# Leaving out the products with a sequence's empty state in a fused Mamba-2 and routed-attention kernel, with PSUM banks given out as pairs or singles

## The chip, the cores and the metric

One core of a Trainium2 chip runs the whole kernel. The time is the device time of one execution in microseconds (us), lower is better. Engines are named as in the profile: PE is the matrix engine (PEld its weight loads), DVE the vector engine, ACT the scalar engine, POOL the general one, SP the queue that issues most DMAs.

## The reference

Eight sequences of 1024 tokens, 512 wide. After a layer norm, two branches are added to the input: a Mamba-2 block and a routed attention. Cut to what matters for the change:

```python
def step(state, inp):                      # one token
    dA_t, dt_t, x_t, B_t, C_t = inp
    state = state * dA_t[:, :, None, None] + (dt_t[:, :, None] * x_t)[..., None] * B_t[:, None, None, :]
    y = jnp.einsum('bhpn,bn->bhp', state, C_t)
    return (state, y)
init = jnp.zeros((Bsz, NHEADS, HEADDIM, D_STATE), x.dtype)
_, ys = jax.lax.scan(step, init, xs_scan)
y = ys.transpose(1, 0, 2, 3) + D[None, None, :, None] * xs
y = y.reshape(Bsz, L, D_INNER) * jax.nn.silu(z)
y = y * jax.lax.rsqrt(jnp.mean(y * y, -1, keepdims=True) + EPS) * gamma
return x + y @ out_proj_w.T
```

The state is zero at the start of each sequence, and what it is after a sequence's last token is used by nothing.

## The kernel before, in words

The program has two halves, one after the other. The Mamba half comes first; the attention half follows, and the change does not touch its code.

**Blocks and chunks.** The 8192 tokens are 16 blocks of 512 (`NBLK`), each of 4 chunks of 128 (`CK`), so 64 chunks (`NCH`), eight to a sequence (`TPS`). Block i+1 is prepared while the chunks of block i run: its rows are normed and turned (`turn`), its router logits and step sizes made (`logits`, `dt`, `cum`), and ten convolutions done (`conv`: products on PE, `raw`, `tap0` and a tanh on ACT, three taps (L1412) and the last product `conv_silu` (L1418) on DVE, into the tile xsT).

**One chunk.** The PE steps are: `open` (L1046 and L1050, transposes of xsT), `inter` (L1086, state times C: what the sequence so far gives to this chunk), `proj` of the chunk before (L1104), `intra` (L1114, the chunk with itself), `gram` of the next chunk (L1057), `z` of the next chunk in two halves (L1067 and L1069), `state` (L1095, what this chunk adds to the state), `gate` (L1076, transposes of the gated result). Between `intra` and `gate` lies a chain on three engines, called the y chain below: `y2` (L1482, DVE), `yz` (L1488, DVE), `square` (L1857, ACT), `mean` (L1492, DVE), `root` (L2016, POOL), `y_high` (L1861, ACT), `y_low` (L1496, DVE). Beside them stand `y_in` (L1461, DVE, takes `inter`'s result), `y_skip` (L2012, POOL), `decayed` (L2007, POOL, the old state times its decay), `xw` (L2000, POOL), and `state_out` (L1469, DVE, adds the product `state` to the decayed state; at a sequence's end L1471 writes zeros instead).

**What sets the order.** Every engine runs its own list in order and waits on semaphores. The lists come from a planner that runs while the kernel is built: `make_plan` weaves the steps of PE (`back` with the convolutions and turns of later blocks, at shares that `Part` and `CONV_START, CONV_END` set), and `arrange` hands them with costs in microseconds and dependencies to `Order`, which places the steps of the other engines by due times and gives each PE step its PSUM banks. Before the change, `Order` keeps the eight banks apart: banks 0 to 3 are two pairs, for `open`, `inter`, `intra`, `state` and `gate`; banks 4 to 7 are singles. A PE step that gets a bank waits until the last reader of that bank's former content is done (`wait_given_back`).

## Time and profile before

| what | value |
|---|---|
| runs | 4119.1, 4124.62, 4128.99 us (median 4124.62) |
| profiled execution, its own time | 4083.68 us |
| its span | 4082.2 us |
| PE, DVE, ACT, POOL busy | 89%, 74%, 63%, 45% of the span |
| PE weight loads busy | 53% |
| Mamba half | to about 2008 us |
| top-k search between the halves | to about 2116 us |
| attention half | 1966 us, from there to the end |

The span runs from the first instruction to the last. A busy PE row has a modelled end, so how long a step occupies PE is read from start to start. What stands in square brackets behind a row of the timeline is how long its engine was idle before it, and whose work ended that.

### The profile page before, as it was taken

The page shows a single profiled execution, that of the slowest core. Times are in us where ns is not written, and L with a number is a line of the kernel's source. Part 1 is how long each engine was busy: PE and PEld are TensorE (multiplying, and loading weights), DVE is VectorE, ACT ScalarE, POOL GpSimd, SP SyncE. Part 2 cuts the span into 40 slices and gives each one's busy share as a digit, 9 for nine tenths or more (in the row PEclk, how much of TensorE's full clock was granted, in tenths as well). Part 3 has the DMA queues.
Part 4 walks back from the last instruction along what each step waited for, and adds up shares of the span by engine and source line. Part 5 has one row for each costly group of instructions (what it writes and reads, how often), then busy time and mean ns, then how long its engine had stood idle before and what let it go on. Part 6 is the DMA issues. An engine that isn't in the chain of part 4 may idle for free.

```text
span 4082.2 us, 72578 instructions
## 1 busy us (share of the span) xinstructions
PE 3651.9 (89%) x28414; PEld 2154.2 (53%) x28414; DVE 3024.5 (74%) x5404; ACT 2557.8 (63%) x4781; POOL 1830.9 (45%) x1513
## 2 busy tenths in 40 slices
PE   4899999999999999999518899998999989999998
PEld 2455555555555555555305555555555556555555
DVE  4887888888888888877567576776777667777773
ACT  4776676776676767765314666666666566666665
POOL 0232333333333333333214777756555565555455
PEclk8899999999999999999759999999999999999998
DMA  4223232323232233222222433334333343333332
GB/s 124 63 71 78 55 73 71 83 71 84 71 75 59 71 74 76 79 68 44 49 42 66 100 70 75 72 73 101 72 75 65 77 97 68 70 75 75 67 66 37
DMA packets 297669, 294.28 MB, mean 72 GB/s; under 512 B 38663, under 2 KB 223623, under 8 KB 295280
## 3 DMA queue, kind: packets, MB, share of 16 engines
q1 hardware_dynamic: 241008, 186.70, 18.0%
q0 software_dynamic: 56320, 102.94, 14.4%
q8 instruction: 225, 3.69, 0.4%
q14 instruction: 116, 0.95, 0.1%
HBM read 176.19 MB, written 101.71 MB: 68 GB/s over the span
## 4 chain that ended last, share of the span: by engine, by line
PE 62%; DVE 15%; DMA 8%; ACT 6%; issue 5%; POOL 3%; SPq 1%; POOLq 0%; DVEq 0%; ACTq 0%
PE pair L1021 8%; PE pair L1104 7%; PE pair L1267 6%; PE pair L1067 6%; PE pair L1114 5%; DMA xin<-x 3%; PE pair L1184 3%; PE pair L1159 3%; PE pair L1086 3%; DMA rbc<-rank 3%; PE pair L1172 2%; PE pair L1095 2%; PE pair L1200 2%; PE pair L1146 2%; PE pair L1046 2%
## 5 line engine op out<-in xcount | busy, mean ns | idle before, releaser
L1412 DVE SCALAR_TENSOR_TENSOR cv<-raw,taps,cv 128x512 f32<-128x512 f32 x480 | 407.5, 857 | 60.7 <-ACT cv L1809 59.4
L1651 DVE TENSOR_REDUCE smx<-pair 128x2 f32<-128x514 f32 x512 | 346.8, 685 | 140.6 <-PE pair L1200 140.5
L2078 POOL TENSOR_TENSOR ph<-pf,ph 128x512 f16<-128x512 f32 x256 | 323.9, 1268 | 201.5 <-ACT ph L1942 200.2
L1021 PE MATMUL pair<-xhT,whi 128*128 128x512 f16 x1280 | 382.8, 381 | 3.4 <-DVE zs L1454 2.7
L2083 POOL TENSOR_TENSOR ohl<-of,ohl 128x256 f16<-128x256 f32 x256 | 209.3, 818 | 307.9 <-ACT ohl L1947 307.9
L1267 PE MATMUL pair<-whi,oT 128*128 128x512 f16 x1024 | 330.8, 385 | 1.1 <-ACT xq L1903 1.1
L1067 PE MATMUL pair<-whi,xhT 128*128 128x512 f16 x1024 | 327.4, 381 | 2.5 <-ACT raw L1795 2.5
L1590 DVE TENSOR_SCALAR_CACHE_REDUCE rjunk<-rbc,cst 128x640 f16<-128x640 f16 (+1 forms) x192 | 185.5, 966 | 181.8 <-DMA rbc<-rank 179.4
L1104 PE MATMUL pair<-ohi,yT 128*128 128x512 f16 x1024 | 316.5, 381 | 1.1 <-ACT yT L1866 1.1
L1159 PE MATMUL pair<-xq,whi 128*128 128x512 f16 x1024 | 312.7, 388 | 0.7 <-ACT xk L1903 0.7
L1839 ACT ACTIVATE de<-de,cum 128x128 f32<-128x128 f32 x1024 | 312.1, 389 | 1.5
L1939 ACT ACTIVATE pf<-pair 128x1024 f32<-128x1024 f32 x256 | 262.7, 1026 | 44.1 <-PE pair L1229 34.3
L1684 DVE TENSOR_TENSOR ph<-pf,ph 128x512 f16<-128x512 f32 x256 | 277.6, 1085 | 6.0 <-ACT ph L1942 3.8
L1942 ACT CAST ph<-pf 128x1024 f16<-128x1024 f32 x256 | 267.5, 1045 | 8.2
L2007 POOL TENSOR_TENSOR state<-state,decs 128x1024 f32<-128x1024 f32 x63 | 138.8, 2204 | 265.7 <-issue 264.3
L2051 POOL DMA_INDIRECT gat<-rows,slot_i x192 | 185.7, 967 | 155.6 <-DVE slot_i L1600 113.9
L2072 POOL DMA_INDIRECT y<-res,slot_i x128 | 203.3, 1588 | 112.6 <-ACT res L1960 92.9
L1021 PE MATMUL pair<-xhT,wlo 128*128 128x512 f16 x640 | 243.6, 381 | 0.0
L1245 PE MATMUL pair<-nvb,pnT 96*128 96x65 f16 x1024 | 202.0, 197 | 45.7 <-DVE qa L1615 37.4
L1114 PEld LDWEIGHTS pair<-xdt,de 128*128 128x128 f32 x2048 | 237.7, 192 | 7.8 <-issue 0.8
L1247 PE MATMUL pair<-vhi,ph 128*128 128x65 f16 x2048 | 241.5, 195 | 0.0
L1249 PE MATMUL pair<-vhi,ph 128*128 128x65 f16 x2048 | 241.4, 195 | 0.0
(245 smaller groups left out, 10446.9 us busy)
## 6 DMA issues: line engine op xcount, KB each, us to landing
de<-cum SPq DMA_DIRECT2D x64, 1024.0 KB, 9.4
rows<-rowt SPq DMA_DIRECT2D x16, 1040.0 KB, 12.6
xin<-x SPq DMA_DIRECT2D x16, 1024.0 KB, 12.8
y<-xin SPq DMA_DIRECT2D x16, 1024.0 KB, 4.3
y<-ob POOLq DMA_DIRECT2D x64, 256.0 KB, 4.1
rbc<-rank SPq DMA_DIRECT2D x64, 256.0 KB, 3.6
qb<-qa SPq DMA_DIRECT2D x32, 512.0 KB
wst<-wkv SPq DMA_DIRECT2D x32, 256.0 KB, 3.3
```

The lines of the kernel that those rows point to most:

```text
L1021: ins = pe.matmul(bk[:], w[:, k, ws], xt[:, ha, k, :], start=n == 0, stop=n == 3 * KD - 1)
L1067: pe.matmul(pz[:], xt[:, ha, k, cs], w[:, k, j * 512:(j + 1) * 512], start=n == 0, stop=False)
L1104: ins = pe.matmul(bk[:], yT[:, ha * KI + k, :], w[:, k, :], start=k == 0 and n == 0, stop=k == KI - 1 and n == 2)
L1114: ins = pe.matmul(pw[:, h * HD:(h + 1) * HD], de[ch % 2][:, h, :], xdt[:, h, :], start=True, stop=True)
L1159: ins = pe.matmul(bk[:], w[:, k, ws], xq[:, ha * KD + k, :], start=n_ == 0, stop=n_ == 3 * KD - 1)
L1267: ins = pe.matmul(bk[:], o_[:, ha * KD + k, :], w[:, k, 3 * D:4 * D], start=k == 0 and m == 0, stop=k == KD - 1 and m == 2)
L1412: ve.scalar_tensor_tensor(c_[:], r_[:, t:t + BLK], taps[:, ct, t:t + 1], c_[:], ALU.mult, ALU.add).then_inc(done, 1)
L1651: ve.tensor_reduce(smx[:, qt, 2 * h2:2 * h2 + 2], sc[:, :, 0:NK + 1], AX.X, ALU.max)
L1684: ve.tensor_tensor(p_[:, 1, 0], f[:, 0], p_[:, 0, 0], ALU.subtract).then_inc(S.plv, 1)
L1839: ins = ac.activation(d_[:, h, :], d_[:, h, :], ACT.Relu, bias=cum_t[i % 2][:, c, h:h + 1], scale=-1.0)
L1942: ac.copy(p_[:, 0], f[:]).then_inc(S.ph, 1)
L2078: po.tensor_tensor(p_[:, 1, 1], f[:, 1], p_[:, 0, 1], ALU.subtract).then_inc(S.plp, 1)
```

## The change

A sequence's first chunk (`opens`) no longer has the steps `inter`, `y_in`, `y_skip` and `decayed`: its `y2` adds the product `intra` to the skip term (dxs) at once, and its `state_out` copies the product `state`. A sequence's last chunk (`ends`) no longer has `xw`, `decayed`, `state` and the write of zeros. The counts that semaphores are waited for follow (`fed`, `kept`, `both`). In numbers: 8 of 64 `inter`, 7 of 63 `state`, 8 `y_in`, 8 `y_skip`, 7 `xw`, 15 of 63 `decayed` and 8 writes of zeros fall away.

`Order` may now give any even-odd pair of the eight banks as a pair and any bank as a single; a single prefers a bank whose partner is taken. The share of the convolutions and of the turns in a block is shifted, and the length of a block is now the sum of its own steps.

```diff
-CONV_START, CONV_END = -0.15, 1.1
+CONV_START, CONV_END = -0.05, 1.05
...
-                sets = [(k, k + 1) for k in range(0, BANKS // 2, 2)] if kind == "pair" else [(k,) for k in range(BANKS // 2, BANKS)]
+                sets = [(k, k + 1) for k in range(0, BANKS, 2)] if kind == "pair" else [(k,) for k in range(BANKS)]
...
-                b = min(sets, key=lambda b: max(banks[k][0] for k in b))
+                b = min(sets, key=lambda b: (len(b) == 1 and b[0] ^ 1 not in busy and b[0] ^ 1 not in taken, max(banks[k][0] for k in b)))
...
+def opens(ch):
+
+    return ch % TPS == 0
...
+def ends(ch):
+
+    return (ch + 1) % TPS == 0
...
-            yield ("inter", ch)
-            yield 1.72
+            if not opens(ch):
+                yield ("inter", ch)
+                yield 1.72
...
-                yield ("state", ch)
-                yield 1.72
+                if not ends(ch):
+                    yield ("state", ch)
+                    yield 1.72
...
-            others.append(Part(ahead, 0.5 if i else 0, 2.6))
+            others.append(Part(ahead, 0.5, 2.6) if i else Part(ahead, 0.3, 4.0))
...
-        weave(Feed(back(i), CK * 21.6, record), *others)
+        weave(Feed(back(i), sum(us for us in back(i) if isinstance(us, float)), record), *others)
...
-                ve.memset(state[0][:], 0.0).then_inc(S.new, 1)
...
             def state_out(ch):
                 new = state[(ch + 1) % 2]
-                q.wait_ge(S.st_mm, ch + 1)
-                q.wait_ge(S.sd, ch + 1)
-                if (ch + 1) % TPS:
-                    ve.tensor_tensor(new[:], new[:], bank("state", ch)[:].rearrange("p (h d) -> p h d", h=NH), ALU.add).then_inc(S.new, 1)
+                q.wait_ge(S.st_mm, kept(ch) + 1)
+                got = bank("state", ch)[:].rearrange("p (h d) -> p h d", h=NH)
+                if opens(ch):
+                    q.wait_ge(S.inter_mm, fed(ch))
+                    ve.tensor_copy(new[:], got).then_inc(S.new, 1)
                 else:
-                    ve.memset(new[:], 0.0).then_inc(S.new, 1)
+                    q.wait_ge(S.sd, both(ch) + 1)
+                    ve.tensor_tensor(new[:], new[:], got, ALU.add).then_inc(S.new, 1)
...
-                ve.tensor_tensor(yb[:], yb[:], bank("intra", ch)[:].rearrange("p (h d) -> p h d", h=NH), ALU.add).then_inc(S.y2, 1)
+                if opens(ch):
+                    q.wait_ge(S.yl, ch)
+                    q.wait_ge(S.dxs, ch + 1)
+                else:
+                    q.wait_ge(S.yd, fed(ch) + 1)
+                ve.tensor_tensor(yb[:], dxs[:] if opens(ch) else yb[:], bank("intra", ch)[:].rearrange("p (h d) -> p h d", h=NH), ALU.add).then_inc(S.y2, 1)
```

The change moves instructions too. Three places are shown, first PE at the end of chunk 40, the first chunk of the sixth sequence, as it was: `state`, `gate`, `open` of chunk 41 and its `inter`, one behind the other, then the first row of `proj`.

```order
3173 L1021 MATMUL pair<-xhT,wlo 128x512
3174 L1095 MATMUL pair<-xw,btok 128x512 x2
3175 L1076 MATMUL pair<-id,yhl 128x128 x16
3176 L1046 MATMUL pair<-cst,xsT 128x128 x8
3177 L1050 MATMUL pair<-cst,xsT 128x128
3178 L1086 MATMUL pair<-state,xsT 128x512 x2
3179 L1104 MATMUL pair<-ohi,yT 128x512
```

The same place of the changed kernel, whose lines stand 38 lower in the file: `state` (L1133), `cum`, `gate` (L1114), a convolution (L1059, of which the eight rows are cut to two), `open` (L1084, L1088), `inter` (L1124).

```order
3159 L1133 MATMUL pair<-xw,btok 128x512 x2
3160 L1069 MATMUL pair<-dts,cst 128x16 x4
3161 L1074 MATMUL pair<-cst,dts 16x128 x4
3162 L1114 MATMUL pair<-id,yhl 128x128 x16
3163 L1059 MATMUL pair<-xhT,whi 128x512 x2
3164 L1059 MATMUL pair<-xhT,wlo 128x512
...
3171 L1084 MATMUL pair<-cst,xsT 128x128 x8
3172 L1088 MATMUL pair<-cst,xsT 128x128
3173 L1124 MATMUL pair<-state,xsT 128x512 x2
```

`cum` and a convolution now lie between `state` and the next `open`, which still gets the pair that `state` held. In all, 21 of the 64 `open` get the pair of the `state` before them; with one exception, in the first block, something besides `gate` lies between the two. The other 43 get a pair that other steps held earlier.

The second place is PE at the end of chunk 39, the last of the fifth sequence. Before: the end of `z`, `state`, a `turn`, `gate`, and the start of `logits` (L1008), behind which come `gram`, `open`, `inter`.

```order
3076 L1069 MATMUL pair<-z_bias,ones 128x512
3077 L1095 MATMUL pair<-xw,btok 128x512 x2
3078 L996 MATMUL pair<-id,xh 128x128 x8
3079 L1076 MATMUL pair<-id,yhl 128x128 x16
3080 L1008 MATMUL pair<-shi,xhT 128x24
```

After: `z`, `logits` (L1046 there, 33 rows cut to two), `gate` (L1114), `gram` (L1095), `open`, `proj` (L1142).

```order
3066 L1107 MATMUL pair<-z_bias,ones 128x512
3067 L1046 MATMUL pair<-shi,xhT 128x24
...
3099 L1046 MATMUL pair<-shi,xhT 128x24
3100 L1114 MATMUL pair<-id,yhl 128x128 x16
3101 L1095 MATMUL pair<-xsT 128x128
3102 L1084 MATMUL pair<-cst,xsT 128x128 x8
3103 L1088 MATMUL pair<-cst,xsT 128x128
3104 L1142 MATMUL pair<-ohi,yT 128x512
```

`state` and `inter` are gone, `logits` stands ahead of `gate` instead of behind it, and the last convolution, which stood between `intra` 39 and `z`, now stands ahead of `intra` 39. Between `intra` 39 and `gate` 39 there are now `z`, a turn, `z` and `logits` alone.

The third place is DVE at the same boundary, from `yz` of chunk 39 on, before:

```order
1219 L1488 SCALAR_TENSOR_TENSOR yb<-yb,zs 128x1024
1220 L1412 SCALAR_TENSOR_TENSOR cv<-raw,taps,cv 128x512
1221 L1492 TENSOR_SCALAR yn<-yn 128x1
1222 L1412 SCALAR_TENSOR_TENSOR cv<-raw,taps,cv 128x512 x2
1223 L1418 SCALAR_TENSOR_TENSOR xsT<-xsT,cv 128x512
1224 L1496 SCALAR_TENSOR_TENSOR yhl<-yb,yn,yhl 128x1024
1225 L1412 SCALAR_TENSOR_TENSOR cv<-raw,taps,cv 128x512
1226 L1471 MEMSET state 128x1024
1227 L1454 SCALAR_TENSOR_TENSOR zs<-zs,pair 128x512
1228 L1418 SCALAR_TENSOR_TENSOR xsT<-xsT,cv 128x512
1229 L1449 TENSOR_TENSOR gmask<-pair,cst 128x128
1230 L1369 TENSOR_SCALAR logit<-pair,nrm 128x8 x4
```

And after, where L1407 and L1408 read the result of `logits`, L1542 is `y_low` and L1456 `conv_silu`:

```order
1147 L1534 SCALAR_TENSOR_TENSOR yb<-yb,zs 128x1024
1148 L1450 SCALAR_TENSOR_TENSOR cv<-raw,taps,cv 128x512
1149 L1456 SCALAR_TENSOR_TENSOR xsT<-xsT,cv 128x512
1150 L1538 TENSOR_SCALAR yn<-yn 128x1
1151 L1456 SCALAR_TENSOR_TENSOR xsT<-xsT,cv 128x512
1152 L1494 SCALAR_TENSOR_TENSOR zs<-zs,pair 128x512
1153 L1407 TENSOR_SCALAR logit<-pair,nrm 128x8 x4
1154 L1408 SCALAR_TENSOR_TENSOR dts<-pair,dt_b 128x64
1155 L1542 SCALAR_TENSOR_TENSOR yhl<-yb,yn,yhl 128x1024
1156 L1494 SCALAR_TENSOR_TENSOR zs<-zs,pair 128x512
1157 L1416 SCALAR_TENSOR_TENSOR dts<-dts 128x64
1158 L1469 TENSOR_TENSOR decs<-de,cum 128x16
```

The last `conv_silu` of the block stands further ahead, and `y_low` stands behind the two instructions that need the result of `logits`.

On SP, in the blocks that open a sequence, the load of the rows for the block after next (L2122) stood behind the load for the decays of the next block's third chunk (L2141) and now stands right behind the store (L2126) on which it waits. In the attention half the order of all PE steps is unchanged; some get another bank than before.

## Rows read from the trace of the kernel before

**Rows 1.** The page: busy us, share of the span and instructions of each engine.

```profile
PE 3651.9 (89%) x28414; PEld 2154.2 (53%) x28414; DVE 3024.5 (74%) x5404; ACT 2557.8 (63%) x4781; POOL 1830.9 (45%) x1513
```

**Rows 2.** Windows: stretch, its length, busy us by engine, PEclk, DMA share, GB/s.

```profile
851.00:1084.00 233.00, 226.05 (x1368) 128.40 (x1368) 194.35 (x269) 164.38 (x365) 82.14 (x52) 1.00 0.30 73
1820.00:2010.00 190.00, 167.46 (x897) 94.64 (x895) 119.59 (x121) 92.12 (x199) 51.37 (x34) 0.95 0.21 38
```

**Rows 3.** Waits of PE from 120 to 1990 us: total us, times, longest.

```profile
PE pair L1046 <- DVE state L1469: 33.4, 45, 3.2
PE pair L1046 <- DVE xsT L1418: 32.5, 16, 12.7
PE pair L1076 <- DVE yhl L1496: 10.1, 4, 4.7
```

**Rows 4.** Timeline of PE: start, us, engine, line, operation, idle time before it.

```profile
143.39 1.97 PE L1046 MATMUL pair<-cst,xsT 128*128 128x128 f32 x8 [12.73 <-DVE xsT L1418]
1378.71 1.09 PE L1046 MATMUL pair<-cst,xsT 128*128 128x128 f32 x8 [0.42 <-DVE state L1469]
```

**Rows 5.** Timeline of PE from chunk 7's `intra` to chunk 8's `proj`.

```profile
368.35 0.59 PE L1021 MATMUL pair<-xhT,whi 128*128 128x512 f16 x2
...
370.94 0.38 PE L1067 MATMUL pair<-whi,xhT 128*128 128x512 f16 x1
...
373.94 0.62 PE L996 MATMUL pair<-id,xh 128*128 128x128 f16 x8
...
377.40 1.99 PE L1095 MATMUL pair<-xw,btok 128*128 128x512 f32 x4
379.23 0.61 PE L996 MATMUL pair<-id,xh 128*128 128x128 f16 x8
379.67 1.06 PE L1076 MATMUL pair<-id,yhl 128*128 128x128 f16 x16
380.57 0.18 PE L1008 MATMUL pair<-shi,xhT 128*128 128x24 f16 x1
...
381.77 0.47 PE L1057 MATMUL pair<-xsT 128*128 128x128 f32 x2
...
384.26 1.88 PE L1086 MATMUL pair<-state,xsT 128*128 128x512 f32 x4
385.98 0.38 PE L1104 MATMUL pair<-ohi,yT 128*128 128x512 f16 x1
```

**Rows 6.** Instructions of `inter` on PE: count, ns min/median/max.

```profile
L1086 PEld LDWEIGHTS pair<-state,xsT x256: 186/191/338, 145.2 to 1982.0; 128*128 128x128 f32 x128
```

**Rows 7.** Timeline from 1344 to 1353 us, chunks 40 and 41.

```profile
1344.08 2.47 DVE L1337 BATCH_NORM_STATS2 stats<-xin 128x6 f32<-128x512 f32 x4 [3.00 <-DMA xin<-x]
1348.34 1.09 PE L1046 MATMUL pair<-cst,xsT 128*128 128x128 f32 x8 [3.19 <-DVE state L1469]
1349.38 3.58 PE L1086 MATMUL pair<-state,xsT 128*128 128x512 f32 x4
```

**Rows 8.** A window behind that wait; PEclk is the third number from the end.

```profile
1350.00:1352.00 2.00, 2.00 (x4) 0.76 (x3) 1.93 (x6) 1.53 (x4) 1.35 (x2) 0.50 0.00 0
```

**Rows 9.** Timeline: y chains of chunks 38 and 63, and readers of `logits`.

```profile
1271.73 1.17 PE L1114 MATMUL pair<-xdt,de 128*128 128x64 f32 x9
...
1274.50 1.21 DVE L1482 TENSOR_TENSOR yb<-yb,pair 128x1024 f32<-128x1024 f32 x1
1283.34 1.28 DVE L1496 SCALAR_TENSOR_TENSOR yhl<-yb,yn,yhl 128x1024 f16<-128x1024 f32 x1 [0.17 <-ACT yhl L1861]
...
1317.29 0.61 DVE L1369 TENSOR_SCALAR logit<-pair,nrm 128x8 f32<-128x8 f32 x4
1317.83 0.21 DVE L1370 SCALAR_TENSOR_TENSOR dts<-pair,dt_b 128x64 f32<-128x64 f32 x1
...
1991.74 1.22 DVE L1482 TENSOR_TENSOR yb<-yb,pair 128x1024 f32<-128x1024 f32 x1 [7.41 <-PE pair L1114]
...
1998.79 1.89 PE L1076 MATMUL pair<-id,yhl 128*128 128x128 f16 x16 [7.08 <-DVE yhl L1496]
```

More of the change, by code:

```diff
@@ L295, in run, with fed, kept, both @@
         plan.now = now
+def opens(ch):
+    return ch % TPS == 0
+def ends(ch):
+    return (ch + 1) % TPS == 0
+def fed(ch):
+    return ch - (ch + TPS - 1) // TPS
+def kept(ch):
+    return ch - ch // TPS
+def both(ch):
+    return sum(1 for c in range(ch) if not opens(c) and not ends(c))
 def chain(*gens):
@@ L381, in last, with state_before @@
         return step if step[1] >= 0 else None
+    def state_before(ch):
+        return last(("state", ch - 2 if ends(ch - 1) else ch - 1))
     def conv_of(i, k):
@@ L405, in arrange @@
         elif name == "inter":
-            add("PE", 1.72, step, [last(("state_out", a - 1))], [("pair", [("y_in", a)])])
+            add("PE", 1.72, step, [("state_out", a - 1)], [("pair", [("y_in", a)])])
         elif name == "state":
@@ L458, in arrange @@
         add("DVE", 2.6, ("mask", ch), [("decay", ch), ("gram_out", ch)])
[L459 to L465 removed]
+        add("ACT", 0.25, ("open_b", ch), [("open", ch), state_before(ch)])
+        add("DVE", 1.22, ("xdt", ch), [("open", ch), last(("intra", ch - 1))] + ([] if ends(ch - 1) else [("xw", ch - 1)]))
+        add("DVE", 1.22, ("dxs", ch), [("open", ch), last(("y2" if opens(ch - 1) else "y_skip", ch - 1))])
+        if not ends(ch):
+            add("POOL", 2.0, ("xw", ch), [("xdt", ch), ("dec", ch), state_before(ch)])
+            if not opens(ch):
+                add("POOL", 2.5, ("decayed", ch), [("dec", ch), ("state_out", ch - 1)] + ([] if opens(ch - 1) else [("inter", ch - 1)]))
+                add("DVE", 1.22, ("state_out", ch), [("state", ch), ("decayed", ch), ("inter", ch)])
+            else:
+                add("DVE", 1.22, ("state_out", ch), [("state", ch), last(("inter", ch - 1))])
         for j in range(2):
@@ L468, in arrange @@
             add("DVE", 0.69, ("z_silu", ch, j), [("z_tanh", ch, j)])
-        add("DVE", 1.22, ("y_in", ch), [("inter", ch), ("cum_exp", i), last(("y_low", ch - 1))])
-        add("POOL", 2.7, ("y_skip", ch), [("y_in", ch), ("dxs", ch)])
-        add("DVE", 1.22, ("y2", ch), [("intra", ch), ("y_skip", ch)])
+        if opens(ch):
+            add("DVE", 1.22, ("y2", ch), [("intra", ch), ("dxs", ch), last(("y_low", ch - 1))])
+        else:
+            add("DVE", 1.22, ("y_in", ch), [("inter", ch), ("cum_exp", i), ("y_low", ch - 1)])
+            add("POOL", 2.7, ("y_skip", ch), [("y_in", ch), ("dxs", ch)])
+            add("DVE", 1.22, ("y2", ch), [("intra", ch), ("y_skip", ch)])
         add("DVE", 1.23, ("yz", ch), [("y2", ch), ("z_silu", ch, 0), ("z_silu", ch, 1)])
@@ L524, in back @@
             yield 1.26
[L525 to L526 removed]
+            if not opens(ch):
+                yield ("inter", ch)
+                yield 1.72
             if ch:
```

47 lines of the change are left out of this document (23 added, 24 removed).

## The prediction

> **What bounds the kernel now.** I read the page's head first, then windows by stage, then PE's waits, then the timeline at the waits. Of the span of 4082.2 us the page has PE busy for 89%, DVE for 74% [rows 1]; the windows [rows 2] split that. A sequence in the middle of the Mamba half (233 us) has PE busy for 226.05 us, DVE for 194.35, ACT for 164.38, POOL for 82.14, at full clock: PE is the bound there, and 7 us a sequence are its idle time. The stretch with the last block (190 us, PE 167.46) has PE waiting too, and the attention half is untouched code.
>
> What PE waits for [rows 3] is nearly all in front of `open` (L1046): 33.4 us in 45 waits for `state_out`, and 32.5 us in 16 waits for the last `conv_silu`. The first is not a data dependence: `open` reads xsT, but it gets the pair of banks that `state` wrote and `state_out` still reads. Its usual size is 0.42 us [rows 4]; where it is larger, DVE stood before a load of rows, as at 1344 us: 3.00 us for xin, then `state_out`, and `open` 3.19 us late [rows 7]. Of the second kind 12.73 us is the start-up [rows 4], where ten convolutions in a row are bound by DVE and ACT; the 15 others sum to 32.5 - 12.7 = 19.8 us, 1.3 each on average.
>
> One rule speaks against counting PE's busy time. PE's weight loads are busy for 128.40 of 233 us only [rows 2]. The Trainium skill, "Perfetto Trace Analysis", section Identifying the Most-Contended Engine, holds that matmul busy share is no good measure and that weight loads are one; taken so, `inter` would cost only its four loads of 0.191 us [rows 6], 0.8 us, and 15 removed products 11.5 us. The trace disagrees: `inter` starts at 384.26 and the next product at 385.98 [rows 5], so 1.72 us of PE's order passes. I count that.
>
> **The change part by part.** All terms are for the profiled execution (4083.68 us, span 4082.2) and are then put on the median.
>
> *Products gone from PE.* `state` takes 379.23 - 377.40 = 1.83 us, `inter` 1.72 [rows 5]. Seven of each: 12.8 and 12.0. The eighth `inter`, in the start-up, took 3.58 us or so at the low clock (as the one at 1349.38 did [rows 7]), but without it PE reaches `intra` sooner and waits there for `xdt` and the mask: between 0 and 3.6, I take 1.5. Sum **-26.3**.
>
> *Work gone from DVE and POOL* (`y_in`, the writes of zeros, `decayed`, `xw`, `y_skip`): nothing, since these engines are covered by PE (194.35 and 82.14 beside 226.05 us [rows 2]). Where that cover is thin, at a boundary, it is in the terms below.
>
> *Waits for `state_out`.* With all eight banks in one pool, 43 `open` get other pairs, and 20 of the other 21 have a convolution, `cum` or `logits` beside `gate` between `state` and themselves. A convolution is 370.94 - 368.35 = 2.6 us, `logits` 381.77 - 380.57 = 1.2 us [rows 5], both more than the 0.42 missing. The rows' load moves ahead on SP by a chunk or more, so the large ones should go too. At least nothing, at most 33.4; I take **-30**.
>
> *Waits for `conv_silu`.* At a sequence's start the last convolution is now ahead of `intra`, and `conv_silu` further ahead on DVE; inside a sequence the distance on PE is as before, but ACT and DVE reach it sooner in their lists. Between 0 and 19.8; I take **-15**. The 12.73 us of the start-up I leave.
>
> *A new wait at a sequence's end.* This is what is late next. Between the end of `intra` and `gate` PE had a convolution, `z`, a turn, `z`, `state` and a turn: 379.67 - 368.35 = 11.3 us. Now it has `z` (373.94 - 370.94 = 3.0), a turn with the second `z` (377.40 - 373.94 = 3.46) and `logits` (1.2) [rows 5]: 7.7 us. The y chain needs 1998.79 - 1991.74 = 7.05 us with nothing beside it, and 1284.62 - 1274.50 = 10.1 us in a full chunk, both from `y2`'s start [rows 9]. And `y_low` stands on DVE behind the readers of `logits`, which end 0.61 + 0.21 us after it, then 1.28 us of its own and two hand-overs: 2.3 us after `logits` [rows 9]. The chain alone would give 10.1 + 0.1 - 7.7 = 2.5. Both say the same; behind `gate` are queued `gram`, `open` and `proj`, so PE pays it in full. Seven times 2.3: **+16** (least 0 if `logits`' readers are quick and the chain short; most 7 times 4.3, if the chain takes 12).
>
> *Tighter `gate` elsewhere.* In the middle of a sequence a convolution moved from behind `intra` to before it in about 22 chunks: the distance falls from 13.2 us (two convolutions, two `z`, `state`, and `gram` of 0.2) to 10.6. The chain of 10.1 us [rows 9] fits, but `y2` started late behind other DVE work: its `intra` ends at 1271.73 + 1.17 = 1272.9, 1.6 us ahead, so chain and delay are 11.7 [rows 9]. Left as they are, they would cost 1.1 in each; up to 2 is my upper bound. The changed DVE list has fewer taps between `y2` and `y_low`. Between 0 and 22 x 2 = 44; nearer to the fitting row, 0.4 each: **+9**.
>
> *The clock.* After the wait of 3.19 us `inter` took 3.58 us and PEclk was 0.50 in the window at 1350, the lower level of 1.2 GHz [rows 7, 8], where the same step takes 1.72 at the upper [rows 5]. That costs 1.8 us. Three such places of the kernel before should go, -5. In their place stands the new wait of 2.3 us at seven boundaries, with `logits`' tiny products before it and transposes after: 0 to 12.6, I take half, +6. Together **+1**.
>
> *Hidden.* The last block's `gate` waits (10.1 us in all [rows 3]) come from the y chain and keep their order: 0. The attention half keeps its order; a bank more or less far back in time: 0. `dxs` to `y2` at a sequence's start: `intra` comes later than `dxs`, 0. The longest new queue on DVE, row statistics ahead of mask and `xdt` at a sequence's start, is 3 us and lies under `proj` (5.2) and a convolution; it costs its excess if the rows' load is late.
>
> Sum: -26.3 - 30 - 15 + 16 + 9 + 1 = **-45.3 us**. The profiled execution is 1% under the median of the runs shown (4083.68 to 4124.62); scaled, -46. So 4124.6 - 46 = **4079 us**.
>
> **The rivals.**
>
> *All bubbles go* (chance 0.17). The repeated 0.42 us is what a shortage of banks looks like, and both new `gate` waits may be absent, if DVE's list is as well arranged as the planner meant. Then -26.3 - 33.4 - 19.8 - 5 = -84.5 at most, 4040; with half of the new wait, 4048 to 4060. For it: every wait of 0.42 has one releaser. Against it: `y_low` behind the readers of `logits` is in the program. The Trainium skill says the same of a gap that repeats on the saturated engine ("Perfetto Trace Analysis", Optimization Strategy: it can mean too little PSUM for the next tile); the trace agrees on the cause, with 45 such waits.
>
> *Only the products' own time* (0.16). The waits move rather than vanish: `open` finds its banks, but `gate` waits instead, at 22 chunks about 1.5 us more. -26.3 - 30 - 15 + 16 + 33 + 1 = -21, range -10 to -28: 4097 to 4115. For it: the chain with its delay is 10 to 12 us wide and the room is now 10.6. Against: the removed DVE work.
>
> *The y chain becomes the bound* (0.06, the other side). If chain and late start come to 12.7 us in those 22 chunks and in ten others like them, the price is 32 x 2.1 = 67 us; with the boundaries' 30 in place of 16 and the clock's 1 the sum is -71.3 + 30 + 67 + 1 = +27, or 4152. It decides from 11.9 us on, where 32 x 1.3 = 41 us close the sum at zero. The rows give 10.1 for the chain and 11.7 with the delay, so it is near but not reached.
>
> *It doesn't reach the time* (0.06): gains and new waits cancel within 8 us. The order shows that the products are gone, so this needs the same mechanism at half its size.
>
> **How the numbers follow.** The forecast, -28 to -62, has 0.55. The range takes in the third case to 4112 and of the second what lies near: 4050 to 4112 leaves out about 2 in 10. 0.2% is 8 us, about what a measurement here can tell from no change. Faster: 0.55 + 0.17 + 0.16 = 0.88; same 0.06; slower 0.06.
>
> **What would show it.** In the changed kernel's profile: `inter` and `state` 56 times each, 224 rows of each on PE; PE's waits before `open` for `state_out` a few us in all; those for the last `conv_silu` near 13 + 5; a new group of `gate` (L1114) waiting for `y_low` with about 2.3 us at seven places and small ones elsewhere; a sequence of 226 to 229 us in place of 233; the attention half as long as before. I am wrong if `gate` waits sum to over 50 us, if DVE still waits for xin at each block's start, or if the attention half moves by more than 5 us through its new banks.

## The result

The changed kernel takes 4065.3 us (median of 6, 4055.0 to 4075.0) against 4124.3 us (6 runs) before: ratio 0.9856 [0.9839, 0.9874], 59 us less. The forecast was 46 less. The profiled execution took 4068.72 us, its span 4067.4.

### The profile after

The page's row of busy time: PE has 60 products fewer and is still busy for the same total, of a shorter span.

```profile
PE 3653.6 (90%) x28354; PEld 2153.8 (53%) x28354; DVE 2973.1 (73%) x5388; ACT 2550.9 (63%) x4781; POOL 1774.5 (44%) x1483
```

The Mamba half ends with the last row of `proj`. Its instructions in the kernel before (first fence) and in the changed one (second fence), with ns min/median/max, first and last start:

```profile
L1104 PE MATMUL pair<-ohi,yT x1024: 378/379/635, 172.8 to 2008.2; 128*128 128x512 f16 x171
```

```profile
L1142 PE MATMUL pair<-ohi,yT x1024: 379/379/634, 174.4 to 1941.4; 128*128 128x512 f16 x171
```

So this half became 66.8 us shorter (63.4 and 64.5 against the ends of the kernel before in runs 7 and 1, 2004.8 and 2005.9); the medians show 59 of it, and 62 in run 2 below, whose Mamba half is the same. I use its end as the measure from here on: the attention half took 1987.4 us in the one profile (from the first top-k turn to the end) and 2039.7 in the other, and runs 1, 2 and 7 below show that this is not the change.

Windows of the changed kernel that answer to [rows 2] (a sequence, then the last block; columns as there). The sequence is 226.2 us in place of 233; PE is busy for 223.95 of them, so 2.3 us of idle time are left of 7.

```profile
812.20:1038.40 226.20, 223.95 (x1365) 128.43 (x1364) 192.20 (x267) 164.22 (x365) 73.90 (x48) 0.99 0.33 76
1753.00:1943.00 190.00, 171.74 (x947) 97.72 (x944) 120.07 (x126) 98.22 (x217) 53.86 (x34) 0.96 0.20 39
```

The largest of PE's waits from 120 us to the end of the half, which answer to [rows 3], and some small ones: total, times, longest. `open` (L1084) waits for `state_out` once, 0.6 us, where it was 33.4 in 45. What was the largest other group, `open` for `conv_silu` (L1456), is now start-up but for 0.75 us at chunk 60; the 12.7 us for `xh` are start-up too, and new. `gate` (L1114) is on top. The last of its twelve, 7.08 us, is the tail that stood there before too [rows 9].

```profile
PE pair L1114 <- DVE yhl L1542: 29.7, 12, 7.1
PE pair L1034 <- DVE xh L1398: 12.7, 2, 8.6
PE pair L1084 <- DVE xsT L1456: 6.2, 2, 5.5
PE pair L1124 <- ACT yT L1912: 1.2, 7, 0.2
PE pair L1084 <- DVE state L1513: 0.6, 1, 0.6
```

The timeline at the end of chunk 39 (the second place that the section on the change shows): the last product of `logits`, its two readers on DVE, `y_low`, `gate`. Seven sequence ends have this wait of 2.04 us. The readers and `y_low` run without a gap, and PE starts 0.06 us after `y_low` ends.

```profile
1274.77 0.17 PE L1046 MATMUL pair<-shi,xhT 128*128 128x24 f16 x1
1274.98 0.63 DVE L1407 TENSOR_SCALAR logit<-pair,nrm 128x8 f32<-128x8 f32 x4 [0.62 <-PE pair L1046]
1275.52 0.21 DVE L1408 SCALAR_TENSOR_TENSOR dts<-pair,dt_b 128x64 f32<-128x64 f32 x1
1275.65 1.27 DVE L1542 SCALAR_TENSOR_TENSOR yhl<-yb,yn,yhl 128x1024 f16<-128x1024 f32 x1
1276.98 1.89 PE L1114 MATMUL pair<-id,yhl 128*128 128x128 f16 x16 [2.04 <-DVE yhl L1542]
1278.66 0.74 PE L1095 MATMUL pair<-xsT 128*128 128x128 f32 x2
```

`gate` then takes 1278.66 - 1276.98 = 1.68 us, where it took 0.90 in [rows 5]. The windows behind two of the seven waits say why: PEclk, third from the end, is 0.50, the 1.2 GHz level, with PE busy throughout.

```profile
372.00:374.00 2.00, 1.97 (x17) 1.97 (x18) 2.00 (x6) 0.30 (x2) 0.00 (x0) 0.50 0.00 0
1504.00:1506.00 2.00, 2.00 (x13) 2.00 (x12) 1.97 (x6) 1.24 (x3) 0.00 (x0) 0.50 0.00 0
```

### The profile page after: what moved, and what is told of

Read it like the earlier page. It is cut to its first block, busy times and chain, and to the rows that moved or that the text cites. A ratio compares the mean times of both kernels' runs of the same rounds, so it can differ in the third digit from the quotient of the medians.

```text
span 4067.4 us, 72426 instructions
## 1 busy us (share of the span) xinstructions
PE 3653.6 (90%) x28354; PEld 2153.8 (53%) x28354; DVE 2973.1 (73%) x5388; ACT 2550.9 (63%) x4781; POOL 1774.5 (44%) x1483
## 3 DMA queue, kind: packets, MB, share of 16 engines
q0 software_dynamic: 56320, 102.94, 14.5%
## 4 chain that ended last, share of the span: by engine, by line
PE 68%; DVE 12%; DMA 5%; ACT 4%; issue 4%; POOL 3%; another core or an unknown queue 2%; SPq 1%; POOLq 0%; ACTq 0%; DVEq 0%
PE pair L1059 10%; PE pair L1142 8%; PE pair L1105 8%; PE pair L1152 6%; PE pair L1305 5%; PE pair L1197 3%; DMA rbc<-rank 3%; PE pair L1133 3%; PE pair L1124 2%; PE pair L1210 2%; PE pair L1222 2%; DVE ph L1730 2%; PE pair L1238 2%; PE pair L1184 2%
## 5 line engine op out<-in xcount | busy, mean ns | idle before, releaser
L1450 DVE SCALAR_TENSOR_TENSOR cv<-raw,taps,cv 128x512 f32<-128x512 f32 x480 | 428.3, 902 | 77.2 <-ACT cv L1855 73.8
L2124 POOL TENSOR_TENSOR ph<-pf,ph 128x512 f16<-128x512 f32 x256 | 308.3, 1206 | 212.8 <-ACT ph L1988 211.7
L1059 PE MATMUL pair<-xhT,whi 128*128 128x512 f16 x1280 | 382.7, 381 | 0.2
L2129 POOL TENSOR_TENSOR ohl<-of,ohl 128x256 f16<-128x256 f32 x256 | 185.3, 724 | 352.9 <-ACT ohl L1993 352.8
L1142 PE MATMUL pair<-ohi,yT 128*128 128x512 f16 x1024 | 318.3, 382 | 1.7 <-ACT yT L1912 1.7
L1993 ACT CAST ohl<-of 128x256 f16<-128x256 f32 x256 | 103.4, 404 | 327.7 <-DVE of L1739 250.8
L1736 DVE RECIPROCAL rden<-pair 128x4 f32<-128x4 f32 x256 | 46.6, 182 | 332.2 <-remote 209.3
L1286 PE MATMUL pair<-vlo,ph 128*128 128x64 f16 x2048 | 244.3, 195 | 0.0
```

The costliest lines, as they stand in the source:

```text
L1059: ins = pe.matmul(bk[:], w[:, k, ws], xt[:, ha, k, :], start=n == 0, stop=n == 3 * KD - 1)
L1142: ins = pe.matmul(bk[:], yT[:, ha * KI + k, :], w[:, k, :], start=k == 0 and n == 0, stop=k == KI - 1 and n == 2)
L1450: ve.scalar_tensor_tensor(c_[:], r_[:, t:t + BLK], taps[:, ct, t:t + 1], c_[:], ALU.mult, ALU.add).then_inc(done, 1)
L2124: po.tensor_tensor(p_[:, 1, 1], f[:, 1], p_[:, 0, 1], ALU.subtract).then_inc(S.plp, 1)
```

## The experiments

Three parts of the change can be set apart: the **products** (steps left out), the **pool** (all eight banks for pairs and singles) and the **shares** (`CONV_START, CONV_END`, the turns' `Part`, the block's length). My theory was that of the prediction: products and pool carry the gain, the shares none of it. The rivals: the attention half gained through its new banks; the gain is the products' own time; the shares do it. Runs 3 to 6, 9 and 10, with before and after, are all eight combinations of the three parts. One thing isn't apart: with products left out the planner finds no order at the old length of a block, so every run without products has the new length, which runs 9 and 10 have by the shares.

All numbers first. "End" is the start of the last `proj` row. PE's busy and idle time are those of the window from 120 us to the end. "Low clock" is what PE lost at the lower clock, summed over windows of 2 us from 150 us on: PE's busy time times (1 - PEclk). Block 0 is from the last row of chunk 0's `open` (L1050, L1088 in the changed kernel) to that of chunk 4's. Each row is one profile. Runs 1 to 4, 5 to 8 and 9 to 12 were timed together, each against the kernel before in the same series (4123.2, 4077.4 and 4124.2 us).

| kernel | ratio | end | busy | idle | low clock | block 0 |
|---|---|---|---|---|---|---|
| before | | 2008.2 | 1797.1 | 92.1 | 14.4 | 121.8 |
| 1 before again | 0.9998 | 2005.9 | 1794.5 | 92.4 | 12.0 | 121.9 |
| 3 products | 0.9931 | 1976.0 | 1779.2 | 77.8 | 25.6 | 120.9 |
| 6 pool | 0.9934 | 1974.9 | 1780.3 | 75.7 | 7.4 | 120.4 |
| 9 shares | 0.9940 | 1982.1 | 1794.4 | 68.6 | 5.6 | 113.1 |
| 4 products, pool | 0.9910 | 1970.8 | 1775.0 | 77.0 | 28.2 | 120.4 |
| 5 products, shares | 0.9962 | 1990.7 | 1791.0 | 81.0 | 32.6 | 120.3 |
| 10 pool, shares | 0.9866 | 1951.0 | 1785.6 | 46.4 | 5.5 | 112.6 |
| after (all three) | 0.9856 | 1941.4 | 1766.9 | 55.5 | 18.1 | 111.7 |
| 11 all, old convolution shares | 0.9877 | 1958.0 | 1766.7 | 72.3 | 19.8 | 117.1 |
| 8 after, `y_low` first | 0.9841 | 1941.5 | 1760.2 | 62.3 | 10.2 | 111.7 |
| 12 after, both dependences | 0.9825 | 1934.4 | 1759.9 | 55.5 | 11.1 | 112.9 |

### 1. The kernel before, once more

No edit.

> The kernel before, unchanged, profiled and timed once more. Theory A (the attention half's length varies from execution to execution, and the first profile of before caught a short one): the new profile has the attention half, from the first product of the top-k turns to the end, at 2010 to 2040 us in place of 1987, and a time near 4124. Theory B (the changed kernel's bank numbers lengthen it): the new profile shows 1987 us again, and the missing 41 us between profile and timed runs lie elsewhere.

Measured: 4124.11 us, 0.9998 [0.9990, 1.0007], theory A. The half ends at 2005.9, the waits are those of [rows 3] within 2.3 us. But the attention half is 2029.1 us long, against 1987.4. So the first profile of before was of a quicker attention half than its timed runs, and that is why it lay 1% under their median. The Mamba half is not touched by it.

### 2. The changed kernel, attention banks numbered as before

After the plan of the attention half is begun, the eight banks are made free in the order that the old planner had:

```diff
+    plan.now = 2000.7200000000134
     plan.append(("attention",))
+    for j, k in enumerate([7, 5, 6, 2, 3, 0, 1, 4]):
+        plan.free[k] = (plan.now - 1.0 + 0.01 * j, plan.free[k][1])
```

> The changed kernel, with the attention half's PSUM banks numbered as in the kernel before, bank for bank; the Mamba half as changed. Theory A (spread of the attention half): the same time as the changed kernel, 4057 to 4073 us. Theory B (the numbers cost 52 us there): about 4013 us. A middle case, the numbers cost some 8 us (4124 - 67 = 4057 against 4065 measured): 4057.

Measured: 0.9853 [0.9836, 0.9870], end 1940.4, attention half 2029.0 us, theory A. The end is the changed kernel's within 1 us, the attention half run 1's. The new bank numbers give and cost nothing.

### 3. Products alone

```diff
-CONV_START, CONV_END = -0.05, 1.05
+CONV_START, CONV_END = -0.15, 1.1
-                sets = [(k, k + 1) for k in range(0, BANKS, 2)] if kind == "pair" else [(k,) for k in range(BANKS)]
+                sets = [(k, k + 1) for k in range(0, BANKS // 2, 2)] if kind == "pair" else [(k,) for k in range(BANKS // 2, BANKS)]
-                b = min(sets, key=lambda b: (len(b) == 1 and b[0] ^ 1 not in busy and b[0] ^ 1 not in taken, max(banks[k][0] for k in b)))
+                b = min(sets, key=lambda b: max(banks[k][0] for k in b))
-            others.append(Part(ahead, 0.5, 2.6) if i else Part(ahead, 0.3, 4.0))
+            others.append(Part(ahead, 0.5 if i else 0, 2.6))
```

The length of a block stays the sum of its steps, which the missing steps need.

> Products, write of zeros and their companions left out as in the change, but pairs and singles kept apart and the old shares of the convolutions and turns; the length of a block is the sum of its steps, since with the old length the planner finds no order. Theory (the terms of the prediction add): the 15 products give 26 us, waits before open stay at about 33 + 20, the wait of gate at a sequence's end may appear: Mamba half 20 to 30 us shorter, about 4100. Rival (the order does it all, the products are hidden by what waits next): within 8 us of before.

Measured: 0.9931 [0.9914, 0.9947], end 30 to 32 us earlier. PE's waits to 1955 us, in the kernel with the products alone:

```profile
PE pair L1114 <- DVE yhl L1542: 32.3, 17, 2.5
PE pair L1084 <- DVE xsT L1456: 10.9, 1, 10.9
PE pair L1084 <- DVE state L1513: 9.7, 23, 0.4
```

The gain looks like the products' 26 us, as the theory had it, but its parts are others: the waits of `open` shrink too (65.9 to 20.6 us), and `gate` waits at 17 places and more time at the lower clock (25.6 against 14.4 us) eat into it.

### 4. Products and pool

Of run 3's diff only the first and the last pair of lines (`CONV_START` and `Part`).

```diff
-CONV_START, CONV_END = -0.05, 1.05
+CONV_START, CONV_END = -0.15, 1.1
-            others.append(Part(ahead, 0.5, 2.6) if i else Part(ahead, 0.3, 4.0))
+            others.append(Part(ahead, 0.5 if i else 0, 2.6))
```

> As the products-only kernel, with any free pair or single of the eight banks; old shares of convolutions and turns. Theory: the 45 waits for state_out go, another 25 to 33 us, 4070 to 4080, and the waits for the last conv_silu stay near 20 - 5. Rival (the shares are what removes the waits): no more than 10 us better than products only.

Measured: 0.9910 [0.9895, 0.9926], end 1970.8. By my sum these two parts are nearly the whole; they give 35 to 37 us of 67, and only 5 more than the products alone, so the rival's number holds, though the pool does take waits away. `open` waits for `state_out` for 3.4 us in place of 9.7, but idle time is that of run 3 (77.0 us against 77.8): `gate` waits as long as there, and new are 8.9 us in the start-up (for `xh`) and 8.1 in front of `intra` (L1152), for which the profile shows no releaser.

```profile
PE pair L1114 <- DVE yhl L1542: 32.3, 17, 2.5
PE pair L1084 <- DVE xsT L1456: 10.6, 1, 10.6
PE pair L1034 <- DVE xh L1398: 8.9, 1, 8.9
PE pair L1152 <- issue: 8.1, 6, 1.7
PE pair L1084 <- DVE state L1513: 3.4, 8, 0.4
```

### 5. Products and shares

Of run 3's diff only the two middle pairs (the banks apart again).

```diff
-                sets = [(k, k + 1) for k in range(0, BANKS, 2)] if kind == "pair" else [(k,) for k in range(BANKS)]
+                sets = [(k, k + 1) for k in range(0, BANKS // 2, 2)] if kind == "pair" else [(k,) for k in range(BANKS // 2, BANKS)]
```

> The changed kernel, but with pairs kept to banks 0 to 3 and singles to banks 4 to 7: products left out and new shares. Theory A (the pool of eight banks is what removes the waits, the prediction's step): 25 us or more above the changed kernel, about 4090, with about 45 short waits of open for state_out. Theory B (after the runs on products alone and with the pool: the shares of convolutions and turns carry the rest, the pool a few us): within 10 us of the changed kernel, 4065 to 4075, block 0 at 112 us in place of 121.

Measured: 0.9962 [0.9950, 0.9974], end 1990.7: neither theory, and a half that is longer than with either part alone. Waits of this kernel:

```profile
PE pair L1114 <- DVE yhl L1542: 29.7, 12, 7.1
PE pair L1059 <- DVE cum L1461: 13.3, 6, 2.2
PE pair L1105 <- ACT xhT L1819: 6.1, 6, 1.0
PE pair L1084 <- DVE state L1513: 4.5, 11, 0.4
```

`gate` waits exactly as in the changed kernel. New is a convolution (L1059) that gets the bank of `cum` and waits for its copy, once in six sequences. Each of these six waits and the seven of `gate` at sequence ends is followed by the lower clock, here. PE is busy 24 us longer than in the changed kernel with the same instructions: 14.5 of it is the lower clock (32.6 against 18.1 us), the other 9.6 I can't place.

### 6. Pool alone

```diff
-                sets = [(k, k + 1) for k in range(0, BANKS // 2, 2)] if kind == "pair" else [(k,) for k in range(BANKS // 2, BANKS)]
+                sets = [(k, k + 1) for k in range(0, BANKS, 2)] if kind == "pair" else [(k,) for k in range(BANKS)]
-                b = min(sets, key=lambda b: max(banks[k][0] for k in b))
+                b = min(sets, key=lambda b: (len(b) == 1 and b[0] ^ 1 not in busy and b[0] ^ 1 not in taken, max(banks[k][0] for k in b)))
```

> The kernel before with the pool of eight banks alone: all products kept, old shares. Theory A (the prediction): the 33 us of waits before open for state_out go, 4090 to 4100. Theory B (the pool moves the waits elsewhere): 4112 to 4124, waits of open for state_out gone or small, but others in their place, at gate, at intra or at the start-up.

Measured: 0.9934 [0.9922, 0.9946], end 31 to 33 us earlier: theory A's time, and the size of the term for `state_out`, with theory B's moved waits inside. The waits of this kernel to 1954 us:

```profile
PE pair L1046 <- DVE xsT L1418: 29.8, 12, 14.1
PE pair L1076 <- DVE state L1469: 15.4, 11, 1.4
PE pair L1046 <- DVE state L1469: 1.7, 4, 0.4
```

Half of the 33.4 us has moved from `open` to `gate`, which now gets `state`'s pair in eleven places. Of the 33.3 us against before, 16.4 are idle time and 7.0 the lower clock; the other 9.8 are busy time of the same instructions, which I can't place. So the term's size is met by other things than the term.

### 7. The kernel before, attention banks numbered as after

```diff
-                banks = self.seat(kind)
+                banks = (7,) if step == ("v", 1, 1) else self.seat(kind)
     plan.append(("attention",))
+    for j, k in enumerate([0, 1, 3, 6, 7, 4, 5, 2]):
+        plan.free[k] = (plan.now - 1.0 + 0.01 * j, plan.free[k][1])
```

> The kernel before, with the attention half's PSUM banks numbered as in the changed kernel, bank for bank; the Mamba half as before. Theory A (the numbers cost nothing): 4124. Theory B (they cost 5 to 10 us, what the changed kernel's 4065 stands above 4124 - 67 and above the same kernel with the old numbers, 4061): 4129 to 4134, with the attention half about 2035 us in the profile.

Measured: 1.0002 [0.9993, 1.0011] against the kernel before of its series, theory A. With run 2 this ends the rival of the banks, from both sides.

### 8. `y_low` ahead of the readers of `logits`

In the plan only; the computation is the same.

```diff
-        add("DVE", 0.8, ("logits_out", i), [("logits", i)] + ([("cum_copy", i - 1), ("raw", i - 1, CONVS[-1])] if i else []))
+        add("DVE", 0.8, ("logits_out", i), [("logits", i)] + ([("cum_copy", i - 1), ("raw", i - 1, CONVS[-1])] if i else []) + ([("y_low", CK * (i - 1) - 1)] if i > 1 and ends(CK * (i - 1) - 1) else []))
```

> The changed kernel, with one dependence more in the planner: the readers of logits stand on DVE behind y_low of a sequence's last chunk, so that y_low no longer waits for them. Theory A (the wait of 2.04 us of gate at seven sequence ends comes from that place in DVE's list alone): the wait goes, 14 us less, 4051. Theory B (the y chain itself is nearly as late: y_high ends 1.1 us before y_low starts): each wait falls to about 1.0 us, 7 us less, 4058.

Measured: 0.9841 [0.9828, 0.9853], from another series than the changed kernel's 0.9856; the half ends at 1941.5, where it ended before this edit. Of its waits:

```profile
PE pair L1114 <- DVE yhl L1542: 22.2, 12, 7.1
PE pair L1059 <- DVE cum L1461: 13.3, 6, 2.2
```

The seven waits fell from 2.04 to 0.98 us, as theory B had it: the order on DVE was half of them, and what is left is the y chain itself. The time at the lower clock fell by 8 us. Both were given back by run 5's wait for the copy of `cum`, 13.3 us, so theory B's 7 us don't show in the half. None of its six waits is followed by the lower clock here, where all were in run 5 (see the last section).

### 9. Shares alone

```diff
-CONV_START, CONV_END = -0.15, 1.1
+CONV_START, CONV_END = -0.05, 1.05
-            others.append(Part(ahead, 0.5 if i else 0, 2.6))
+            others.append(Part(ahead, 0.5, 2.6) if i else Part(ahead, 0.3, 4.0))
-        weave(Feed(back(i), CK * 21.6, record), *others)
+        weave(Feed(back(i), sum(us for us in back(i) if isinstance(us, float)), record), *others)
```

> The kernel before with the new shares and block length alone: all products, banks apart. Theory A (the shares fit only where the banks are one pool, as products and shares without it lost 15 us of Mamba half against products alone): Mamba half at or above that of before, 2005 to 2025 us to its last projection, time at or above before. Theory B (the shares help by themselves, about 8 us of block 0 alone): 8 us or more under before.

Measured: 0.9940 [0.9922, 0.9957], end 24 to 26 us earlier. Theory B: the part that my sum left at nothing is worth nearly as much alone as the others. Block 0 is 8.7 us shorter, and the waits of `open` are gone with the banks still apart; 23.0 us of waits of the convolution for `z_silu` stand in their place, each up to 1.9 us:

```profile
PE pair L1021 <- DVE zs L1454: 23.0, 12, 1.9
PE pair L1086 <- ACT yT L1866: 12.8, 16, 2.3
PE pair L1046 <- DVE state L1469: 1.3, 3, 0.4
```

The waits of `open` for `conv_silu`, 32.5 us in 16 before, are 1.0 in 2 here and still 29.8 in 12 in run 6. In run 3, under the old shares, they are 10.9 in 1, all start-up. What runs 3 and 9 have in common is the new length of a block; no run changes it alone.

### 10. Pool and shares

The diffs of runs 6 and 9 together; all products are computed.

```diff
-CONV_START, CONV_END = -0.15, 1.1
+CONV_START, CONV_END = -0.05, 1.05
...
+                sets = [(k, k + 1) for k in range(0, BANKS, 2)] if kind == "pair" else [(k,) for k in range(BANKS)]
```

> The kernel before with the pool of eight banks and the new shares, all products kept. Theory A (pool and shares belong together, and the products then add their own 26 to 30 us): Mamba half to about 1970 us, as with the pool alone or a few us better, ratio to before 0.991 to 0.993. Theory B (the shares pay only with the products gone): above 1980 us.

Measured: 0.9866 [0.9847, 0.9886], end 1951.0. Neither theory had this (A said about 1970, B above 1980). These two do 55 to 57 us of the 67, and here they add up (run 6 had 31 to 33, run 9 24 to 26). All waits above 1 us up to 1930 us:

```profile
PE pair L996 <- DVE xh L1360: 12.3, 2, 7.3
PE pair L1076 <- DVE yhl L1496: 8.3, 4, 2.5
PE pair L1086 <- ACT yT L1866: 6.9, 12, 0.6
PE pair L1046 <- DVE xsT L1418: 5.8, 2, 5.1
PE pair L1086 <- ACT xhT L1773: 1.5, 1, 1.5
```

No sequence end has a `gate` wait of over 0.2 us: three of these four lie in the last block, one in the first. And the lower clock costs 5.5 us, with run 9's 5.6 the least of all.

Why `gate` doesn't wait at a sequence's end is in the rows of the end of chunk 39. Its `intra` ends at 1268.19, `y_low` (L1496) 10.2 us later, `gate` (L1076) starts 12.4 us after `intra`: the y chain has 2.1 us to spare. In the kernels without products PE has only `z`, a turn, `z` and `logits` there, 7.7 us.

```profile
1277.10 1.28 DVE L1496 SCALAR_TENSOR_TENSOR yhl<-yb,yn,yhl 128x1024 f16<-128x1024 f32 x1
1280.55 1.05 PE L1076 MATMUL pair<-id,yhl 128*128 128x128 f16 x16
```

Of the difference `state` is 1.8 us, less than the 2.1; the larger part is a convolution of 2.6 us, which in this kernel stands behind `intra` and in every kernel without products ahead of it, under old and new shares alike.

### 11. All parts, convolution shares as before

```diff
-CONV_START, CONV_END = -0.05, 1.05
+CONV_START, CONV_END = -0.15, 1.1
```

> The changed kernel with the convolutions' old start and end (-0.15, 1.1), and the new share of the turns in the first block and the new block length. Theory A (the turns' share is what shortens the first block, 120 to 112 us, and the convolutions' what shortens the others by 1 to 2 us each): Mamba half to 1955 to 1963 us, block 0 near 112. Theory B (the convolutions' shares do all of it): 1970 us, block 0 near 120.

Measured: 0.9877 [0.9858, 0.9896], end 1958.0: theory A's end, but not its first block, which is 117.1 and not 112. These two numbers alone are worth 17 us: `gate` waits for `y_low` in 19 places for 42.0 us in place of 12 and 29.7 (six of them new in the middle of sequences, 1.32 us each at chunks 11, 19 and so on to 51), and block 0 is 5.4 us longer. From run 4 this kernel differs in the turns' share of the first block alone, and its half ends 12.8 us earlier. PE is busy for as long as in the changed kernel; it is all idle time.

### 12. Run 8 with the copy of `cum` ahead of `xdt`

```diff
-        add("DVE", 1.22, ("xdt", ch), [("open", ch), last(("intra", ch - 1))] + ([] if ends(ch - 1) else [("xw", ch - 1)]))
+        add("DVE", 1.22, ("xdt", ch), [("open", ch), last(("intra", ch - 1))] + ([] if ends(ch - 1) else [("xw", ch - 1)]) + ([("cum_copy", i + 1)] if ch % CK == 1 and i + 1 < NBLK else []))
```

> The changed kernel with the readers of logits behind y_low at a sequence's end, and besides the copy of cum ahead of xdt of a block's second chunk on DVE. Theory A (the wait of 2.2 us of a convolution for the copy of cum, six times in the kernel with the first dependence alone, is a place in DVE's list): it goes, and with the 7 us of the first the Mamba half ends about 1928, ratio to before about 0.981 to 0.982. Theory B (waits on PE move on to the next place, since DVE's list is what is short of room): no better than 1938.

Measured: 0.9825 [0.9808, 0.9843], 4052.94 us against 4124.19; end 1934.4, between the two theories and 7.0 us ahead of the changed kernel. It is the quickest half of all, though by total time its interval still overlaps that of the changed kernel. Its waits:

```profile
PE pair L1114 <- DVE yhl L1542: 15.5, 12, 2.5
PE pair L1124 <- ACT yT L1912: 6.0, 6, 1.0
PE pair L1114 <- DVE state L1513: 2.7, 7, 1.4
```

The wait for `cum` is gone. Idle time is 55.5 us as in the changed kernel, since `inter`'s 6.0 for `yT` are new; the 7 us come from the clock (11.1 against 18.1 us lost), and how far that is the edit's work is open (see the last section).

## Why the prediction was right, and where by luck

The side, the range and the likeliest case held; the measured 59 us lie near the end of the forecast's 28 to 62. The sum was made for the Mamba half, where -45.3 stands against -66.8 measured in profiles. Point by point:

- **Products gone, -26.3**: right for PE's order. `inter` and `state` have 224 rows each. Busy time less what the lower clock cost fell by (1797.1 - 14.4) - (1766.9 - 18.1) = 33.9 us, of which run 10, with all products, has 2.6; the rest is 31. The same difference is 29 from before to run 3, 26 from run 6 to run 4 and 30 from run 9 to run 5. These figures carry the modelled ends of the rows, and between the four kernels with all products they differ by up to 16 us themselves, so 26 start to start stands. Priced by weight loads, which the prediction set against this, they would be 11.5 us, and the rows speak against it; the page of the Trainium skill that it took this from ("Perfetto Trace Analysis", section Identifying the Most-Contended Engine) speaks of how close a kernel is to its roofline, not of the price of a step.
- **Waits for `state_out`, -30**: measured -32.8. The large ones went as forecast: DVE waited for `xin` ten times, 16.2 us, from 150 to 2000 us before, and never in the changed kernel's half. Run 6 shows that the pool takes them from `open`, but moves half of them to `gate` under the old shares. Run 9 loses them too with the banks still apart, so the pool isn't the only way, as the prediction had it.
- **Waits for `conv_silu`, -15**: the 15 outside the start-up went from 19.8 to 0.7 us, -19. They were not alike, as "1.3 each" had them: the one at chunk 4 was 5.24 us, the others about 1.
- **New wait at a sequence's end, +16**: measured 7 x 2.04 = 14.3, at the places forecast. Of the two ways to the number that "say the same", the readers of `logits` are the one at work; the chain alone, put at 2.5, gives 0.98 (run 8), since it takes 8.6 us from the end of `intra` and not 10.1. That both agreed was luck.
- **Tighter `gate` elsewhere, +9**: nothing. The other waits of `gate` are 0.7 us in block 0 and the last block's. The room did shrink, to 10.45 to 10.99 us in 21 chunks where it had been 12.98. But `y_low`, which in these chunks ended 11.7 to 12.6 us after `intra`, now ends 9.2 to 10.2 us after it: the late start of `y2`, mostly 1.6 to 1.9 us, is 0.04 to 0.7, and the chain from there is at most 10.1. The rows of chunk 41 below have 0.04, 9.6 and a `gate` 10.5 us behind `intra`, which ends at 1321.95. Under the old convolution shares six chunks in the middle of sequences do wait (run 11).

```profile
1321.99 1.22 DVE L1528 TENSOR_TENSOR yb<-yb,pair 128x1024 f32<-128x1024 f32 x1 [0.26 <-PE pair L1152]
1330.29 1.28 DVE L1542 SCALAR_TENSOR_TENSOR yhl<-yb,yn,yhl 128x1024 f16<-128x1024 f32 x1 [0.96 <-ACT yhl L1907]
1332.49 1.06 PE L1114 MATMUL pair<-id,yhl 128*128 128x128 f16 x16
```

- **The clock, +1**: +3.7 (18.1 against 14.4 us), out of two parts that I had half the size: all seven new waits are followed by the lower clock, from run 10 to the changed kernel +12.6 in place of +6, and without them the pool and the shares save 8.9 in place of 5.
- **The start-up, 0**: `open` of chunk 0 comes 2.85 us later (1.5 against run 1), since turns that stand ahead of it now wait too, as the rows below of the changed kernel show beside [rows 4].

```profile
130.13 1.03 PE L1034 MATMUL pair<-id,xh 128*128 128x128 f16 x8 [4.10 <-DVE xh L1398]
139.74 1.03 PE L1034 MATMUL pair<-id,xh 128*128 128x128 f16 x8 [8.58 <-DVE xh L1398]
146.24 1.97 PE L1084 MATMUL pair<-cst,xsT 128*128 128x128 f32 x8 [5.46 <-DVE xsT L1456]
```

The step that failed is "tighter `gate` elsewhere", 9 us for a thing that doesn't happen and the largest single miss of the sum: a late start of `y2` read in the old order was carried into the new one. Behind it is the reading of the shares as an edit that only shifts waits. They had no term of their own. Run 9 gives them 24 to 26 us alone, run 11 gives 17 to the two numbers for the convolutions. Block 0 is 10.1 us shorter in the changed kernel and 8.7 in run 9; 5.24 of this is the wait at chunk 4, which stands in the term for `conv_silu`, and about 1 the waits for `state_out`; of the first block as such the prediction said nothing. The rival in which all bubbles go was half true: the bubbles of before went, and the new one stayed.

Luck is in the total. Products and pool, the two parts that the sum rests on, give 30 to 33 us each alone, near their terms, but 35 to 37 together. The shares, at nothing in the sum, add 29 on top of them. So the time came out within the range although the parts don't add as the sum has them.

The second thing that the sum hides is what the products are worth here. Leaving them out shortens the half by 30 to 32 us alone and by 4 with the pool (run 6 to 4), lengthens it by 9 with the shares (run 9 to 5), and shortens it by 9.6 with both (run 10 to the changed kernel), where the ratios (0.9866 and 0.9856) can't tell the two apart. In this last pair PE's busy time falls by 18.7 us: 31 for the rows of the products, less 12.6 for the lower clock. Idle time rises by 9.1, mostly 14.3 for the seven waits of `gate`, less 5.7 as `inter` waits less for `yT` (6.9 to 1.2).

So at a sequence's end `inter` and `state`, 3.55 us, go, and 2.04 of waiting and 1.8 (12.6 / 7) of lower clock come. They don't come from the products' cover alone. `inter` never stood over the y chain, and `state`'s 1.8 us would have left run 10's chain covered, with 2.1 us to spare. It is the convolution of 2.6 us that the planner puts ahead of `intra` once the steps are gone, and `y_low` behind the readers of `logits` (half of the wait, run 8). No run moves the convolution alone, so its share is worked out from these rows and not shown. The prediction had the convolution, `state` and the readers in its term for the wait, but set the term beside the whole sum and not beside the products.

Why the three parts don't add (32, 33 and 26 us alone, 66.8 together; 37, 18 and 57 in pairs) is shown as far as the waits: each order of steps has its own shortage. Part of it can be the clock, which doesn't follow from the waits, as the last section says. What makes the lists of runs 4 and 5 fall into other waits I did not follow further. In the Trainium skill, "Perfetto Trace Analysis", section Matmul Optimizations, the advice is to use all eight PSUM banks for parallelism between instructions. The runs agree on its sign (run 6, 0.9934) and show its limit: with products gone under the old shares it gave 5 us (run 3 to run 4).

## What to carry over

When a step is taken out of the engine that bounds a kernel, and a planner makes the order, add up what stands over each dependent chain before and after, moved steps included: here 3.55 us of products went and 2.04 us of waiting and 1.8 us of lower clock came, and of the cover that was lost the larger part is a convolution that moved. A delay read in the old order isn't one of the new order. Where a change brings a resource and a schedule together, the schedule needs a term of its own, and the first block one beside the steady ones. Measure a stage by its own end in the trace when another stage varies between series.

## What was not expected of the hardware

**The attention half has two lengths for one program.** In the first profile of before and in the four of the series in which before took 4077 us, it is 1978.4 to 1991.5 us long; in the eight profiles of the series in which before took 4123 to 4124, it is 2025.5 to 2032.9, and in the changed kernel's own 2039.7. The Mamba half of before ends at 2004.8 to 2008.2 in its three profiles of both kinds. Runs 1 to 4 and 5 to 8 were on the same chip, so it isn't a property of one. The waits of DVE in this half differ in the reciprocal of the softmax sums; the first fence is the kernel before in its first profile, the second is run 1 (the profile calls the releaser remote, as it finds none on the core).

```profile
DVE rden L1690 <- PE pair L1249: 167.2, 127, 5.1
```

```profile
DVE rden L1690 <- remote: 191.9, 46, 6.2
DVE rden L1690 <- PE pair L1249: 123.8, 106, 5.8
```

What makes it so was not tried and stays open.

**A short wait can cost as much again in clock, and whether it does can't be read from the wait.** In the changed kernel all seven waits of 2.04 us, which come behind 48 small products of `logits`, are followed by PEclk 0.50 to 0.58, and each such stretch costs PE about 1.7 or 3.4 us. The small products alone don't do it: in run 10 they stand ahead of `gate` too, without a wait, and no lower clock follows. But the same wait behind the same steps is followed by the lower clock at 7 of 7 places in runs 2, 3 and 5, at 5 of 7 in run 11 and at 3 of 7 in run 4; the one of 0.98 us in runs 8 and 12 at 3 of 7 each. The convolution's wait of 2.22 us for the copy of `cum`, behind the same `gate`, `open`, `inter` and `proj`, is followed by it at 6 of 6 places in run 5 and at none of 6 in run 8. The first row below is behind such a wait in run 5, the second in run 8, both with PE busy throughout.

```profile
535.00:537.00 2.00, 2.00 (x6) 0.71 (x5) 1.93 (x3) 0.00 (x0) 0.00 (x0) 0.50 0.03 6
527.00:529.00 2.00, 2.00 (x16) 1.51 (x14) 1.93 (x3) 0.77 (x2) 0.00 (x0) 1.00 0.03 8
```

What decides it no run shows. With six waits at 1.7 us, some 10 us in the column "low clock" hang on it, so differences of a few us between two kernels' ends are not the edit's for certain.
